# Second chunk of edges in dense tiles: 438 gathers in place of 488, and sums by items of a tile and a block

## The chip, the cores and the metric

One core of a Trainium2 chip runs the whole kernel in one launch. The metric is the device time of that launch in microseconds (us), by the slowest core, and here there is only one.

## What is computed

The reference takes x (6250 nodes of 256 numbers) and 100,000 edges, src and dst. It normalises x, and then adds three things to it: a graph layer, a small attention-like mixer over 8 heads, and at the end a mixture of 8 experts. The graph layer is what this case is about:

```python
def _L0_gnn_ref(x, W1, b1, W2, b2, edge_index):
    dst = edge_index[0]
    nbr = edge_index[1]
    agg = jax.ops.segment_sum(x[nbr], dst, num_segments=n)
    cnt = jax.ops.segment_sum(jnp.ones((nbr.shape[0],), x.dtype), dst, num_segments=n)
    mean = agg / jnp.maximum(cnt, 1.0)[:, None]
    return x @ W1.T + b1 + mean @ W2.T + b2
...
edge_index = jnp.stack([src, dst])
x = x + _L0_gnn_ref(xn, ...) + _L0_mix_ref(xn[None], ...)[0]
x = x + _L0_ffn_ref(_layernorm(x)[None], ...)[0]
```

So row dst[e] of a table is fetched for each edge e and added to the sum of node src[e].

## The kernel before

**Stages.** `edges` normalises x, multiplies it with W2 (by linearity W2 can come before the mean) and stores the products as a table of 6272 rows in HBM, `tab` ("xn_parts", 512 f16 numbers, 1 KB a row). It then sorts the edges on the chip and sums the fetched rows. `nodes` finishes the layer, normalises and routes; `experts` runs the eight experts.

**Sorting.** The 100,000 edges lie as 125 partitions by 800 columns and are handled in two chunks, of 352 and of 448 columns (44,000 and 56,000 edges). A block is 128 nodes, and there are NB = 49 blocks. Each edge of a chunk gets a place: a tile and a lane of 128. A block begins on a new tile, so a chunk has room for 49 partly empty tiles: `chunk_plan` (L46) makes 392 tiles for the first chunk (T0 = 392) and 488 for the second. Places that no edge has hold zeros after the sort, which stands for row 0 of the table; behind the last block's last tile whole tiles are left over. By the numbers, 56,000 edges fill 437.5 tiles, and with half a tile lost in each of 49 blocks some 462 of the 488 hold edges.

The steps of a sort are: count (L638, mask products), `place` (L963, VectorE: running sums, where each block's tiles begin), `rank` (L990), `split`, one column after another (L677 on TensorE, L1101 and L1106 on VectorE, L569 on ScalarE), and `decode` (L1025), which leaves `idx`, the table's row for each place, and `srcl`, the node's lane in the block. `buck` says for each tile which block it is of.

**Summing.** For tile t GpSimd issues one indirect DMA (L471), which fetches 128 rows of 1 KB into one of RING = 32 slots in SBUF; even tiles have their slots in G2 (named w in the profile, since the slots lie in a weight buffer), odd ones in G. It waits for the tile 32 before to be summed. TensorE (`sum_tile`, L684) waits for the slot, and multiplies the tile by a one-hot of `srcl` (S, made by VectorE at L926 for eight tiles at a time) in two matmuls, L697 and L698, into one of four PSUM banks. VectorE (`tile`, L932) adds the bank to the block's sums in XA (L947), at an address from a register; 16 such registers are loaded with one instruction (L936).

```python
    def slot(t):
        return (G, G2)[t % 2], t % RING // 2 * GW
...
        for t in range(TILES):
            if t in (0, T0):
                pool.wait_ge(s_dec, 1 if t == 0 else 2)
            if t >= RING and t % 2 == 0:
                pool.wait_ge(s_tile, t + 2 - RING)
```

**What runs beside the sums.** While the first chunk is summed, its tiles carry the sort of the second: `side_plan` (L107) lists the steps with a cost each and spreads them over the first T0 - RING = 360 tiles. While the second chunk is summed, tiles 16 to 287 of it carry the mixer's head statistics, between tiles 287 and 288 the mixer's matrix is folded into W1 (`key_values`, L1159), and tiles 288 to 483 carry, four tiles to a block, the product of the 49 blocks of x with that W1 ("own": L773, L779, L781 on TensorE, L584 and L587 on ScalarE, L1193 and L1196 on VectorE). For L1196 x is loaded again, by SyncE (L430), up to four blocks ahead.

## Time and profile before

| | |
|---|---|
| median of 3 runs | 2108.47 us (2102.12 to 2109.26) |
| profiled execution, its own time | 2104.35 us |
| its span in the profile | 2102.7 us |
| first gather of the first chunk | 333.4 us into the span |
| gathers of the second chunk | 858.2 to 1492.0 us |
| last add of the second chunk | 1507.1 us |
| busy, of the span | TensorE 75%, VectorE 65%, GpSimd 49%, ScalarE 34% |

Times in the profile count from the span's start. Engines are PE (TensorE), PEld (its weight loads), DVE (VectorE), ACT (ScalarE), POOL (GpSimd), SP (SyncE); a name with q is the engine's instruction queue, where register, semaphore and DMA-issuing instructions show, which are not counted as busy. L471 is line 471 of the kernel before.

### The profile page before, as it was taken

How to read it: one execution, taken by the hardware profiler on the slowest of the kernel's cores; microseconds unless marked ns; L12 is line 12 of the kernel's file. 1: busy time of each engine (PE TensorE's matmuls, PEld its weight loads, DVE VectorE, ACT ScalarE, POOL GpSimd, SP SyncE). 2: the span in 40 equal slices, each digit the busy share in tenths (PEclk: the TensorE clock that was granted, in tenths of full speed). 3: DMA queues.
4: the chain of work that ended last, by engine and by line, in shares of the span. 5: the costliest groups of instructions: out<-in, count | busy, mean ns of one | idle time of the engine just before them, and what ended most of it. 6: DMA issues, size and time to landing. Idle time of an engine off the chain costs nothing. (4 is left out here: it accounts for less than half of the span.)

```text
span 2102.7 us, 24562 instructions
## 1 busy us (share of the span) xinstructions
PE 1578.8 (75%) x6551; PEld 876.4 (42%) x6551; DVE 1362.8 (65%) x3687; ACT 720.3 (34%) x1992; POOL 1023.1 (49%) x1020
## 2 busy tenths in 40 slices
PE   4659896668778875465655667888575799999997
PEld 3434432223333332122222234444374466666665
DVE  6679997789899996466666665555564244444444
ACT  5349992008777873000000001111163122222221
POOL 0000105777777777777777777777336011111111
PEclk9779999679999997555555567766555899999999
DMA  5110162333333335733333344444734422223200
GB/s 150 41 41 21 78 254 63 102 100 96 96 96 101 99 97 103 106 103 102 106 101 103 103 122 124 129 123 114 130 136 159 131 90 89 98 91 101 97 12 5
DMA packets 89244, 210.87 MB, mean 100 GB/s; under 512 B 20674, under 2 KB 49896, under 8 KB 86128
## 3 DMA queue, kind: packets, MB, share of 16 engines
q0 software_dynamic: 51888, 138.08, 25.1%
q1 hardware_dynamic: 35544, 70.56, 10.0%
q8 instruction: 58, 0.95, 0.2%
q10 hardware_dynamic: 1680, 0.67, 0.1%
q14 instruction: 74, 0.61, 0.1%
HBM read 163.98 MB, written 49.89 MB: 102 GB/s over the span
## 5 line engine op out<-in xcount | busy, mean ns | idle before, releaser
L947 DVE TENSOR_TENSOR XA<-XA,bank 128x257 f32 x880 | 368.5, 419 | 341.1 <-PE bank L698 318.8
L471 POOL DMA_INDIRECT G<-xn_parts,idx x440 | 445.3, 1012 | 170.0 <-issue 81.9
L471 POOL DMA_INDIRECT w<-xn_parts,idx x440 | 446.5, 1015 | 134.0 <-issue 134.0
L697 PE MATMUL bank<-G,S 128*128 128x257 f16 x440 | 152.2, 346 | 178.6 <-DMA G<-xn_parts,idx 156.4
L1620 POOL DMA_INDIRECT out<-ob,tok x64 | 66.5, 1039 | 401.3 <-DVE ob L1606 401.3
L697 PE MATMUL bank<-w,S 128*128 128x257 f16 x440 | 151.1, 343 | 138.2 <-DMA w<-xn_parts,idx 120.9
L569 ACT ACTIVATE LV<-LH,v 125x128 f16<-125x128 f16 x600 | 182.6, 388 | 188.0 <-DVE LH L1101 187.7
L1544 PE MATMUL bank<-w,ht 128*117 128x256 f32 (+1 forms) x1024 | 223.7, 379 | 0.0
L1533 PE MATMUL bank<-xt,w 128*128 128x468 f32 (+1 forms) x512 | 215.2, 579 | 0.8 <-ACT xt L1558 0.8
L1544 PEld LDWEIGHTS bank<-w,ht 128*117 128x117 f32 (+1 forms) x1024 | 188.8, 186 | 30.5 <-issue 0.4
L1568 ACT ACTIVATE ht<-bank,b1c 128x468 f32<-128x468 f32 (+1 forms) x128 | 85.6, 669 | 333.8 <-PE bank L1533 333.8
L1597 DVE TENSOR_TENSOR y<-bank,b 128x256 f32<-128x256 f32 (+1 forms) x64 | 27.1, 424 | 235.1 <-PE bank L1544 235.1
L697 PEld LDWEIGHTS bank<-G,S 128*128 128x128 f16 x440 | 46.3, 105 | 311.8 <-DMA G<-xn_parts,idx 277.7
L677 PE MATMUL bank<-HT,LV 125*128 125x488 f16 x600 | 158.6, 372 | 11.3 <-ACT LV L569 9.3
L697 PEld LDWEIGHTS bank<-w,S 128*128 128x128 f16 x440 | 45.8, 104 | 281.1 <-DMA w<-xn_parts,idx 241.1
L698 PE MATMUL bank<-G,S 128*128 128x256 f16 x440 | 155.2, 353 | 0.0
L698 PE MATMUL bank<-w,S 128*128 128x256 f16 x440 | 154.1, 350 | 0.0
L1533 PEld LDWEIGHTS bank<-xt,w 128*128 128x128 f32 x512 | 98.0, 192 | 109.3 <-issue 106.9
L926 DVE TENSOR_TENSOR S<-iota,srcl 128x1024 f16<-128x1024 f16 x110 | 133.8, 1217 | 2.2 <-issue 2.2
L574 ACT ACTIVATE work<-work 128x768 f32<-128x768 f32 (+1 forms) x17 | 13.9, 818 | 351.7 <-DVE work L1139 351.7
L450 POOL DMA_DIRECT2D xn_parts<-G x13 | 10.0, 768 | 237.6 <-DVE G L883 235.7
L563 ACT ACTIVATE LV<-LH,v 125x128 f16<-125x128 f16 x378 | 113.9, 390 | 7.7 <-DVE LH L1070 7.7
(234 smaller groups left out, 2698.1 us busy)
## 6 DMA issues: line engine op xcount, KB each, us to landing
w<-f SPq DMA_DIRECT2D x16, 1024.0 KB, 7.6
expert_rows<-G SPq DMA_DIRECT2D x7, 2048.0 KB, 21.3
xb<-expert_rows SPq DMA_DIRECT2D x8, 1028.0 KB, 11.2
xb<-expert_rows SPq DMA_DIRECT2D x8, 939.7 KB
G<-xn_parts,idx POOLq DMA_INDIRECT x440, 2.8
w<-xn_parts,idx POOLq DMA_INDIRECT x440, 2.8
XA<-x SPq DMA_DIRECT2D x6, 1024.0 KB, 5.7
xn_parts<-G POOLq DMA_DIRECT2D x12, 512.0 KB, 3.6
```

Source lines behind the costliest of these rows:

```text
L471: pool.indirect_dma_start(g[:, o:o + 2 * D], None, tab, bass.IndirectOffsetOnAxis(ap=idx[:, t:t + 1], axis=0)).then_inc(s_g[t % RING], 16)
L563: ins = act.activation(value_slot0(col, n), lane_slots0(col, 1), ACT.Copy, scale=v[0:EP, col:col + 1])
L569: ins = act.activation(value_slot(k, n), lane_slots(k, 1), ACT.Copy, scale=v[0:EP, COLS0 + k:COLS0 + k + 1])
L677: ins = pe.matmul(psV[n][:, 0:CHUNKS[1][3]], value_slot(k, n), tile_slot(k), start=False, stop=False, skip_group_check=True)
L697: pe.matmul(psA[t % AR][:, 0:AGW], lhs, g[:, o + D:o + 2 * D + 1], start=True, stop=True)
L698: pe.matmul(psA[t % AR][:, 0:D], lhs, g[:, o:o + D], start=False, stop=True, skip_group_check=True).then_inc(s_tile, 1)
L926: v.tensor_tensor(S[:, t % SR * P:(t % SR + SB) * P].rearrange("p (j n) -> p j n", n=P), iota_1[:, :].unsqueeze(1).to_broadcast([P, SB, P] ...
L947: v.tensor_tensor(XA[:, ds(o, AGW)], XA[:, ds(o, AGW)], psA[t % AR][:, 0:AGW], ALU.add).then_inc(s_ev, 1)
L1533: ins = pe.matmul(psH[f % 2][:, 0:cols], w1[q][:, k * F + f * P:k * F + (f + 1) * P], xt[n % 2][:, k * TQ * P:k * TQ * P + cols], start=(k ...
L1544: ins = pe.matmul(psY[m % 2][0:rp, 0:D], ht[:, f * TQ * P + m * rp:f * TQ * P + (m + 1) * rp], w2[q][:, f * D:(f + 1) * D], start=(f == 0) ...
L1568: act.activation(ht[:, f * TQ * P:f * TQ * P + cols], psH[f % 2][:, 0:cols], ACT.Relu, bias=b1c[:, e * FT + f:e * FT + f + 1]).then_inc(s_ ...
L1620: pool.indirect_dma_start(out, bass.IndirectOffsetOnAxis(ap=tok[0:rp, s:s + 1], axis=0), ob[0:rp, s * D:(s + 1) * D], None, bounds_check=N ...
```

## The change

The second chunk's edges are placed one behind another, without a new tile for each block: 56,000 edges in DENSE = 438 tiles, all full but the last. A tile can now hold edges of two blocks, so the sum goes by items, one for each pair of a tile and a block in it: ITEMS = 438 + 48 = 486. Both matmuls and the add run once per item, with the one-hot of only that block's lanes. The first chunk stays as it is.

- `place_dense` (VectorE, in place of `place` for this chunk) and `dense_items` (TensorE) work out for each item its tile, its block and its lanes, and for each tile its last item. 12 VectorE instructions become 28. `decode_dense` with `dense_turn` and `dense_pick` brings the sources from the tiles' order into the items' (8 VectorE instructions become 20). The plan's costs for these steps rise, and 2 x GAP = 6 more tiles carry a piece. The one-hots over tiles (L1106 and L677 before) are 440 wide instead of 488.
- In `sum_tile` TensorE takes the slot's address and the number of landed tiles to wait for from registers, which it loads itself, two loads for 16 items.
- The slots are one array in order of tiles.
- SyncE counts: it waits for each tile's landing and adds one to `s_land`, for which TensorE waits; then it waits for the last item of the tile 16 before (a value from a register) and adds one to `s_free`, for which GpSimd waits.
- The loads of x for L1196 move from SyncE to ScalarE, two blocks ahead in place of four.

```diff
-    for cols in (352, 448):
-        tiles = (cols * EP + NB * (P - 1)) // P
+    for cols, padded in ((352, True), (448, False)):
+        tiles = (cols * EP + NB * (P - 1)) // P if padded else -(-cols * EP // P)
...
+T0 = CHUNKS[0][3]
+DENSE = -(-COLS1 * EP // P)
+ITEMS = DENSE + NB - 1
+IW = -(-ITEMS // SB) * SB
+AHEAD = 16
...
-    rank = place + 1
+    rank = place + 3
...
-    costs = [430] * NB + [8000] + [1100] * (NB + RB1) + [700] * 5 + ([1070] + [350] * (LB - 1)) * (COLS1 // LB) + [1300] * REST + [3000]
+    costs = [430] * NB + [3500, 7000, 4000] + [1100] * (NB + RB1) + [700] * 5 + ([1070] + [350] * (LB - 1)) * (COLS1 // LB) + [1300] * REST + [3000]
...
+        if decode < k <= decode + 2 * GAP:
+            k += 1
...
+    ring = kk["w_0"][:, :].bitcast(F16)
+    ring_high = ring[:, D:RING * GW]
+    G2, G = ring[:, 0:GR * GW], ring[:, GR * GW:RING * GW]
...
-        return (G, G2)[t % 2], t % RING // 2 * GW
+        return t % RING * GW
...
-        sp.wait_ge(s_kv, 1)
-        for b in range(NB):
-            if b >= LD:
-                sp.wait_ge(s_x0, b - LD + 1)
-            rows = P if b < NB - 1 else LASTROWS
-            sp.dma_start(xr[b % LD][0:rows, :], x[b * P:b * P + rows, :]).then_inc(s_xr[b % LD], 16)
+        sp.wait_ge(s_rows, 1)
+        last = []
+        for t in range(T0, T0 + DENSE):
+            sp.wait_ge(s_g[t % RING], 16 * (t // RING + 1))
+            sp.sem_inc(s_land, 1)
+            u = t - T0 - AHEAD
+            if 0 <= u < DENSE - RING:
+                if u % GR == 0:
+                    last[:] = nc.values_load_multi_w_load_instructions(
+                        tile_used[:, u:u + GR], engines=[mybir.EngineType.SP], min_val=T0 + 1, max_val=T0 + ITEMS,
+                        skip_runtime_bounds_check_because="a tile is in no more than NB items, the place step counts them")[1]
+                sp.wait_ge(s_tile, last[u % GR] & 1023)
+                sp.sem_inc(s_free, 1)
 
...
-        for t in range(TILES):
+        for t in range(T0 + DENSE):
             if t >= RING and t % 2 == 0:
-                pool.wait_ge(s_tile, t + 2 - RING)
-            g, o = slot(t)
-            pool.indirect_dma_start(g[:, o:o + 2 * D], None, tab,
+                if t < T0 + RING:
+                    pool.wait_ge(s_tile, t + 2 - RING)
+                else:
+                    pool.wait_ge(s_free, t - T0 + 2 - RING)
+            o = slot(t)
+            pool.indirect_dma_start(ring[:, o:o + 2 * D], None, tab,
                                     bass.IndirectOffsetOnAxis(ap=idx[:, t:t + 1], axis=0)).then_inc(s_g[t % RING], 16)
...
+        def again(b):
+            if b >= LD:
+                act.wait_ge(s_x0, b - LD + 1)
+            rows = P if b < NB - 1 else LASTROWS
+            act.dma_start(xr[b % LD][0:rows, :], x[b * P:b * P + rows, :]).then_inc(s_xr[b % LD], 16)
+
+        for b in range(2):
+            again(b)
+
...
+        def dense_items():
+
+            pe.wait_ge(s_ge, 2)
+            pe.matmul(psG[0][:, 0:IW], ones16[0:NB, 0:1].to_broadcast([NB, P]), from_first[0:NB, 0:IW], start=True, stop=True)
+            pe.matmul(psG[1][:, 0:IW], rest16[0:NB, 0:1].to_broadcast([NB, P]), at_first[0:NB, 0:IW], start=True, stop=True)
+            pe.matmul(psV[1][:, 0:IW], rest16[0:NB, 1:2].to_broadcast([NB, P]), at_last[0:NB, 0:IW], start=True, stop=True)
+            pe.matmul(psV[0][0:1, 0:CHUNKS[1][3]], ones16[0:NB, 0:1], from_start[0:NB, 0:CHUNKS[1][3]],
+                      start=True, stop=True).then_inc(s_bk, 1)
+
+        def dense_turn():
+
+            pe.wait_ge(s_ts, 1)
+            for n in range(4):
+                ins = pe.matmul(psG[0][:, n * P:(n + 1) * P], lane_src[:, n * P:(n + 1) * P], ident16, start=True, stop=True)
+            ins.then_inc(s_tr, 1)
+
+        def dense_pick():
+
+            pe.wait_ge(s_trc, 1)
+            for n in range(4):
+                ins = pe.matmul(psG[1][:, 0:IW], src_lane[:, n * P:(n + 1) * P], pick[n], start=(n == 0), stop=(n == 3))
+            ins.then_inc(s_si, 1)
...
         def sum_tile(t):
             if t == 0:
                 pe.wait_ge(s_one, 2)
-            pe.wait_ge(s_g[t % RING], 16 * (t // RING + 1))
+            if t < T0:
+                o = slot(t)
+                pe.wait_ge(s_g[t % RING], 16 * (t // RING + 1))
+            else:
+                i = t - T0
+                if i % GR == 0:
+                    many = min(GR, ITEMS - i)
+                    item[:] = [nc.values_load_multi_w_load_instructions(
+                        row[:, i:i + many], engines=[mybir.EngineType.PE], min_val=low, max_val=high,
+                        skip_runtime_bounds_check_because="an item's tile is one of the DENSE tiles, its slot one of the ring")[1]
+                        for row, low, high in ((item_slot, 0, (RING - 1) * GW), (item_need, 1, DENSE))]
+                o = item[0][i % GR]
+                pe.wait_ge(s_land, item[1][i % GR] & 511)
             if t % SB == 0:
                 pe.wait_ge(s_S, t // SB + 1)
             if t >= AR:
                 pe.wait_ge(s_ev, t - AR + 1)
             lhs = S[:, t % SR * P:(t % SR + 1) * P]
-            g, o = slot(t)
-            pe.matmul(psA[t % AR][:, 0:AGW], lhs, g[:, o + D:o + 2 * D + 1], start=True, stop=True)
-            pe.matmul(psA[t % AR][:, 0:D], lhs, g[:, o:o + D], start=False, stop=True, skip_group_check=True).then_inc(s_tile, 1)
+            pe.matmul(psA[t % AR][:, 0:AGW], lhs, ring_high[:, ds(o, AGW)], start=True, stop=True)
+            pe.matmul(psA[t % AR][:, 0:D], lhs, ring[:, ds(o, D)], start=False, stop=True, skip_group_check=True).then_inc(s_tile, 1)
 
...
+        pe.wait_ge(s_sid, 1)
         for h in range(2):
             pe.matmul(psG[h][:, 0:KW], zero32[:, :], W1[:, 0:KW], start=True, stop=False, skip_group_check=True)
-        for t in range(T0, TILES):
+        pe.wait_ge(s_rows, 1)
+        for t in range(T0, T0 + ITEMS):
...
+            step(v.tensor_tensor(starts[0:NB, 1:2], starts[0:NB, 0:1], lanes[0:NB, 0:1], ALU.add))
+            v.tensor_scalar(from_start[0:NB, 0:tiles], iota_t[0:NB, 0:tiles], starts[0:NB, 0:1], None, ALU.is_ge)
+            wait()
+            step(v.tensor_scalar(starts[0:NB, 2:3], starts[0:NB, 1:2], 1.0, None, ALU.subtract))
+            v.tensor_scalar(from_first[0:NB, 0:IW], iota_t[0:NB, 0:IW], starts[0:NB, 1:2], None, ALU.is_ge)
+            v.tensor_scalar(at_first[0:NB, 0:IW], iota_t[0:NB, 0:IW], starts[0:NB, 1:2], None, ALU.is_equal)
+            wait()
+            v.tensor_scalar(at_last[0:NB, 0:IW], iota_t[0:NB, 0:IW], starts[0:NB, 2:3], None, ALU.is_equal).then_inc(s_ge, 1)
+            yield
...
+            step(v.tensor_scalar(keep, psG[1][:, 0:IW], lanes[:, 0:1], None, ALU.is_le))
+            v.scalar_tensor_tensor(out=item_tile, in0=psG[0][:, 0:IW], scalar=-1.0, in1=iota_t[:, 0:IW],
+                                   op0=ALU.mult, op1=ALU.add)
+            v.tensor_scalar(buck[0:1, T0:T0 + IW], psG[0][0:1, 0:IW], -1.0, float(RW), ALU.add, ALU.mult)
+            wait()
+            v.scalar_tensor_tensor(out=keep, in0=psV[1][:, 0:IW], scalar=lanes[:, 1:2], in1=keep,
+                                   op0=ALU.is_gt, op1=ALU.mult)
+            step(v.scalar_tensor_tensor(out=used16[0:1, :], in0=psV[0][0:1, 0:tiles], scalar=float(T0),
+                                        in1=iota_t[0:1, 0:tiles], op0=ALU.add, op1=ALU.add))
...
+            v.wait_ge(s_ts, 1)
+            for n in range(4):
+                v.tensor_scalar(pick[n], item_tile, lanes[:, 2 + n:3 + n], None, ALU.is_equal)
+            v.wait_ge(s_tr, 1)
+            v.tensor_copy(src_lane, psG[0][:, 0:4 * P]).then_inc(s_trc, 1)
...
+            v.sem_inc(s_rows, 1)
+            v.wait_ge(s_si, 1)
+            v.tensor_tensor(srcl[:, T0:T0 + IW], psG[1][:, 0:IW], keep, ALU.mult).then_inc(s_sid, 1)
```

TensorE at the start of the second chunk's sums, before (L697, L698: the two matmuls of a tile, G and w the slots):

```order
L784 MATMUL bank<-W,zero 128x129 x2
L697 MATMUL bank<-G,S 128x257 [waits tile_added,source_onehot,gathered_8]
L698 MATMUL bank<-G,S 128x256
L697 MATMUL bank<-w,S 128x257 [waits tile_added,gathered_9]
L698 MATMUL bank<-w,S 128x256
```

and now (L777 loads 16 registers, L782 masks one, ISA sets an address):

```order
L882 MATMUL bank<-W,zero 128x129 [waits item_sources]
L882 MATMUL bank<-W,zero 128x129
L777 TENSOR_LOAD v [waits item_rows_ready]
L777 TENSOR_LOAD v
L782 REGISTER_ALU
L788 ISA [waits tile_added,source_onehot,tiles_landed]
L788 MATMUL bank<-w,S 128x257
L789 ISA
L789 MATMUL bank<-w,S 128x256
L782 REGISTER_ALU
L788 ISA [waits tile_added,tiles_landed]
L788 MATMUL bank<-w,S 128x257
```

Three instructions of the queue come to each item, two loads to each 16, and the wait for one slot's own semaphore has become a wait for the count of landed tiles.

SyncE's queue behind its last loads of the sort, before:

```order
L424 DMA cum<-gb 128x256
L430 DMA work<-x 128x256 [waits key_values_in_w1]
L430 DMA work<-x 128x256 x3
L430 DMA work<-x 128x256 [waits x_added_again] x44
L430 DMA work<-x 106x256 [waits x_added_again]
```

and now (a piece from its middle):

```order
L467 REGISTER_ALU [waits tile_summed,gathered_6]
L467 REGISTER_ALU [waits tile_summed,gathered_7]
L464 TENSOR_LOAD pos [waits tile_summed,gathered_8]
L467 REGISTER_ALU
L467 REGISTER_ALU [waits tile_summed,gathered_9]
L467 REGISTER_ALU [waits tile_summed,gathered_10]
```

The 49 loads have left this queue, and for every tile it waits in turn for a landing and for a sum.

## Rows read from the trace of the kernel before

**Rows 1.** The page: the span

```profile
span 2102.7 us, 24562 instructions
```

**Rows 2.** Groups of instructions, POOL, 858.1 to 1493 us

```profile
L471 POOL DMA_INDIRECT G<-xn_parts,idx x244 | 246.5, 1010 | 74.3 <-PE bank L698 40.2 <-issue 34.1
L471 POOL DMA_INDIRECT w<-xn_parts,idx x244 | 239.9, 983 | 74.3 <-issue 74.3
```

**Rows 3.** Timeline of POOL, the second chunk's first and last gather

```profile
858.19 0.95 POOL L471 DMA_INDIRECT G<-xn_parts,idx  x1 [0.30 <-issue]
...
1492.03 0.95 POOL L471 DMA_INDIRECT w<-xn_parts,idx  x1 [0.30 <-issue]
```

**Rows 4.** Stretches: busy us (count) of PE, PEld, DVE, ACT, POOL; clock, DMA share, GB/s

```profile
858.10:1228.70 370.60, 215.20 (x790) 93.48 (x790) 223.16 (x450) 17.67 (x34) 282.79 (x289) 0.52 0.39 105
1228.70:1460.00 231.30, 184.66 (x698) 104.70 (x698) 129.51 (x303) 29.99 (x87) 178.08 (x175) 0.71 0.44 126
1460.00:1508.00 48.00, 35.53 (x107) 17.69 (x106) 20.25 (x46) 3.82 (x11) 25.57 (x25) 0.50 0.81 81
820.00:858.00 38.00, 14.32 (x50) 3.35 (x48) 15.63 (x32) 0.00 (x0) 29.05 (x30) 0.50 0.92 92
500.00:800.00 300.00, 238.52 (x1227) 103.12 (x1226) 277.58 (x739) 236.87 (x782) 232.39 (x223) 1.00 0.35 98
1360.00:1370.00 10.00, 10.00 (x32) 6.00 (x30) 4.59 (x10) 0.89 (x3) 7.56 (x9) 0.50 0.46 132
```

**Rows 5.** Timeline of a gather, its matmuls and its add, mid second chunk

```profile
1003.68 0.94 POOL L471 DMA_INDIRECT G<-xn_parts,idx  x1 [0.30 <-PE bank L698]
...
1006.76 0.40 PE L697 MATMUL bank<-G,S 128*128 128x257 f16 x1 [0.53 <-DMA G<-xn_parts,idx]
...
1007.50 0.42 DVE L947 TENSOR_TENSOR XA<-XA,bank 128x257 f32 x1 [1.15 <-PE bank L698]
```

**Rows 6.** Timeline of the second chunk's last tiles

```profile
1505.72 0.40 PE L697 MATMUL bank<-G,S 128*128 128x257 f16 x1 [1.21 <-DMA G<-xn_parts,idx]
...
1507.09 0.42 DVE L947 TENSOR_TENSOR XA<-XA,bank 128x257 f32 x1 [0.20 <-DVE XA L947]
```

**Rows 7.** The lines of the gather (L471), its time to landing

```profile
  issue: 216.0, 709
...
DMA to landing us min/median/max: 2.6/2.8/15.4
```

**Rows 8.** Queue of DVE: loads of 16 registers (L936)

```profile
L936 DVEq TENSOR_LOAD <-buck x56: 594/1099/1344, 332.6 to 1496.2; - x56
```

**Rows 9.** Queue of DVE: the register instruction before each add (L947)

```profile
L947 DVEq FUSED_REGOPS  x880: 46/46/46, 337.0 to 1507.0; - x176
```

**Rows 10.** Timeline of PE, one "own" block from L779 to L779

```profile
1360.20 1.91 PE L779 MATMUL bank<-W,work 128*128 128x256 f32 x4
...
1365.30 1.91 PE L779 MATMUL bank<-W,work 128*128 128x256 f32 x4
```

**Rows 11.** Timeline of PE, behind key_values, and POOL's gather for the first of them

```profile
1228.68 0.95 POOL L471 DMA_INDIRECT G<-xn_parts,idx  x1 [0.30 <-PE bank L698]
...
1239.03 0.40 PE L697 MATMUL bank<-G,S 128*128 128x257 f16 x1 [5.26 <-DVE mcol L1189]
...
1247.84 1.03 PE L779 MATMUL bank<-W,work 128*128 128x256 f32 x4
...
1250.90 1.03 PE L779 MATMUL bank<-W,work 128*128 128x256 f32 x4
```

**Rows 12.** Issue of L430 by SP

```profile
L430 SPq DMA_DIRECT2D work<-x x49: 258/328/463, 1239.0 to 1477.0; - x49
```

**Rows 13.** Timeline of DVE, `place` of the second chunk

```profile
367.18 1.09 DVE L965 TENSOR_TENSOR_SCAN cum<-onesw,bank 113x448 f32<-113x448 bf16 x1 [0.49 <-PE bank L638]
...
371.48 0.65 DVE L987 TENSOR_SCALAR buck<-bank 1x488 int32<-1x488 f32 x1
```

**Rows 14.** DVE's tile one-hots of the second chunk (L1106)

```profile
L1106 DVE TENSOR_SCALAR HT<-iota_t,tf x300: 327/339/534, 470.5 to 810.9; 125x488 f16<-125x488 f16 x150
```

More of the change, by code:

```diff
@@ L126, with done_at @@
 SIDE, PLACE, RANK, SORT, DECODE = side_plan()
-PLACE_AT = next(t for t in range(T0) if SIDE[t] > PLACE)
-DECODE_AT = next(t for t in range(T0) if SIDE[t] > DECODE)
+def done_at(k):
+    return next(t for t in range(T0) if SIDE[t] > k)
+PLACE_AT, ITEMS_AT, TURN_AT, PICK_AT = (done_at(k) for k in (PLACE, PLACE + 1, DECODE, DECODE + GAP))
 def side_by(t, first, n):
@@ L305, in edges @@
     DI = HT[:, :].bitcast(I32)
-    idx = sb("idx", [P, TILES], I32)
-    srcl = sb("srcl", [P, TILES], F16)
-    buck = sb("buck", [1, TILES], I32)
+    idx = sb("idx", [P, T0 + CHUNKS[1][3]], I32)
+    srcl = sb("srcl", [P, T0 + IW], F16)
+    buck = sb("buck", [1, T0 + IW], I32)
+    lanes = sb("lanes", [P, 6], F32)
+    starts = sb("starts", [P, 4], F32)
+    rest16 = sb("rest16", [P, 2], F16)
+    from_first, at_first, at_last, from_start = (HT[:, n * TMAX:(n + 1) * TMAX] for n in range(4))
+    item_tile = v1[:, 0:IW // 2].bitcast(F16)
+    keep = v2[:, 0:IW // 2].bitcast(F16)
+    used16 = onesw[:, 0:CHUNKS[1][3]].bitcast(F16)
+    item_slot = v1[0:1, EC - IW:EC].bitcast(I32)
+    item_need = v2[0:1, EC - IW:EC].bitcast(I32)
+    tile_used = pos[0:1, 0:CHUNKS[1][3]].bitcast(I32)
+    lane_src, src_lane, ident16 = LV[:, 0:4 * P], LV[:, 4 * P:8 * P], LH[:, 0:P]
+    pick = [HT[:, n * TMAX:n * TMAX + IW] for n in range(4)]
+    assert IW // 2 <= COLS0 and CHUNKS[1][3] <= 4 * P and IW // 2 <= EC - IW
     S = sb("S", [P, SR * P], F16)
@@ L685, in close @@
             ins.then_inc(s_sx, 1)
+        item = []
         def sum_tile(t):
@@ L1091, in second_chunk @@
                 yield
-            place(1, psV[0], psV[1])
+            yield from place_dense()
             yield
```

127 lines of the change are left out of this document (103 added, 24 removed).

## Prediction

> **What bounds the kernel now.** I read the stretches first, then GpSimd's groups, then single tiles in the timeline. The change touches the second chunk's sums, from 858.1 to 1508 us, and the sort steps that ride on the first chunk's. In the second chunk TensorE is busy 215 of 370.6 us, then 185 of 231.3 us, and VectorE less [rows 4]: no compute engine is full. GpSimd issues one indirect DMA after another: 488 of them take 246.5 + 239.9 = 486.4 us, and before each it idles 148.6 / 488 = 0.30 us [rows 2], put down to nothing but its own issue or to a sum long done. It never waits longer. Its pitch is 635.0 / 488 = 1.301 us; an undisturbed gather has 0.95 + 0.30 = 1.25 us [rows 3], and the other 0.05 us is some long ones, met by VectorE's work. TensorE follows: a gather issued at 1003.68 us is multiplied at 1006.76 us behind a wait for the DMA and added at 1007.50 us, 3.8 us after issue [rows 5]. So **the number of gathers times their pitch** bounds this stage, and the tail behind the last one.
>
> That tail is long: the last gather starts at 1492.03 us and the last add at 1507.09 us [rows 3, 6], 15.1 us for what takes 3.8 us elsewhere. From 1460 us the DMA engines are 0.81 busy for 81 GB/s, where before it was 0.39 for 105 GB/s; the same shows at the end of the first chunk, 0.92 for 92 GB/s [rows 4]. These are the stretches in which the left-over empty tiles come, whose 128 lanes all fetch row 0: about 26 of them by the numbers (488 - 462), and the sums then go at the DMA's pace, waiting for it 1.21 us before a tile [rows 6]. I take the empty tiles to be the cause.
>
> **The change, part by part.**
>
> *50 gathers fewer.* If the long ones go in proportion, 50 x 1.301 = 65.1 us; if only undisturbed ones go (VectorE's work per item stays, 486 for 488), 50 x 1.25 = 62.5 us. I take -63.8 us. This counts in full as long as GpSimd sets the pace.
>
> *No empty tiles in the second chunk.* The tail of 15.1 us shrinks. It can't be under 3.8 us; SyncE's hop and the last block's product come on top, and in the stage of the own blocks TensorE runs up to a block late, so I take 7 us: -8 us, with bounds of -11.3 and 0.
>
> *Registers on TensorE.* Two loads for 16 items, and an ALU step and two address steps each. VectorE's load of 16 takes 1.10 us [rows 8], its address step 0.046 us [rows 9]; taken for TensorE, that is 2.2 / 16 + 3 x 0.046 = 0.28 us an item in its queue. Dense, an item comes every 1.301 x 438 / 486 = 1.17 us. In the first 288 items TensorE was busy 0.58 of the time, so 0.65 now, and the queue's part fits even unhidden: 0. In the own stage a block of four items has 4.69 us. Without waits a block takes 5.10 us at the low clock of 1.2 GHz [rows 10] and 3.06 us at 2.4 GHz [rows 11]; the mean granted clock there was 0.71, so 0.42 of the time at the higher level [rows 4]. It ran at 1.2 GHz while it was full from 1360 to 1370 us [rows 4] and got the higher level behind such stretches; a tighter pace leaves fewer waits between them. With everything hidden but half of the loads (0.28 us a block), a block needs 5.38 or 3.34 us, and a third of the time at 2.4 GHz is enough for 4.69 us. I take +2 us for moments when it lags, with bounds 0 and +24 us (first rival). 
>
> *SyncE's counting.* A hop before each sum, some 0.1 to 0.2 us as a wait and a register step cost on VectorE's queue (0.046 us a step [rows 9]), and a load of 1.1 us once in 16 tiles. It delays and doesn't add up, since there are 1.30 us for each tile: 0, and its share of the tail is counted above. Queued behind the wait for a sum is the next landing's count; it would hold TensorE back only with 16 tiles outstanding, and the worst lag was 10.4 us, 8 tiles, behind `key_values` [rows 11]. GpSimd gets a slot back only when the tile 16 later has landed, so it can be 16 ahead: landing takes 2.8 us in the median and 15.4 us at most [rows 7], 12 tiles. No stall of GpSimd from either.
>
> *Loads of x on ScalarE.* 49 issues at 0.33 us by SyncE's row [rows 12]; ScalarE is busy 30 of 231 us there [rows 4], and two blocks ahead are 9 us. 0.
>
> *Sort steps on the first chunk.* 28 more VectorE instructions. `place` took 367.2 to 372.1 us for its 12 [rows 13], 0.4 us each, so some 11 us more, while the tile one-hots get 448 x 0.339 x 48 / 488 = up to 15 us cheaper [rows 14]. VectorE is 0.93 busy there [rows 4], but GpSimd may run 30 tiles ahead, about 40 us, so a lag of 10 to 15 us is covered by the ring. If that cover were gone, the 11 us would be paid. I take +1 us (bounds -3 and +11).
>
> Sum: -63.8 - 8 + 2 + 1 = -68.8 us. The profiled execution had 2104.35 us (span 2102.7 us [rows 1], the rest lies around it), so 2035.6 us. The median of the runs is 4.1 us above that execution: **2040 us**. The later stages are as before.
>
> **Rivals.**
>
> *TensorE bounds the own stage.* Nothing of the register work is hidden and the clock stays where it was: a block takes 5.10 + 1.1 = 6.2 us low and 3.06 + 1.1 = 4.2 us high, together 1 / (0.58 / 6.2 + 0.42 / 4.2) = 5.17 us, against the 4.69 us of the gathers: 49 x 0.48 = 24 us of the gain are given back, 2064 us. For it: the busy share there is already 0.80. Against: the granted clock rose behind full stretches, and at the higher level a block takes 3.06 us [rows 11], so that TensorE soon caught up behind `key_values`.
>
> *Slower than before: loads on TensorE's queue.* TensorE never runs past a register load, and the loads cost it far more than VectorE. The 486 items must then end later than 1507 us. With 288 items at 1.17 us (337 us), the stage breaks even when a block takes (1507 - 858 - 337 - 7) / 49 = 6.2 us all through, so 1.1 us of unhidden register work at the low clock and never the higher one. At three times VectorE's price (6.6 us for two loads, 1.65 us a block, and 0.55 us for the rest) it is 5.10 + 2.2 = 7.3 us: 49 x 1.1 = 54 us over, 2162 us. Against: VectorE loads 16 registers in 1.10 us, and TensorE was at the higher level 0.42 of the time. The Trainium skill (Runtime: NRT & Kernel Launch, "Instruction fetch mechanics") states about 200 ns for each register loaded, so an estimated 3.2 us for 16 and this rival's price; VectorE's row of 1.10 us, 0.07 us a register, speaks against it.
>
> *The gain is lost ahead of it.* VectorE's added steps come on the path of the first chunk (+11 us) and the tail stays (0 for -8): -63.8 + 2 + 11 = -51 us, 2058 us. For it: VectorE is 0.93 busy. Against: GpSimd never waited for a sum there.
>
> *It doesn't do what it says.* If the free counts came so late that GpSimd waits for them, its idle before a gather would exceed 0.30 us; a stall of 0.15 us a gather for 406 gathers would take 61 us back: no change, 2101 us. It needs landings of over 20 us, and the longest is 15.4 us.
>
> **How the numbers follow.** Forecast 0.70, TensorE-bound 0.13, lost ahead 0.08, no change 0.02, slower 0.07. The range takes in the forecast's bounds (-65.1 - 11.3 - 3 gives 2029 us) and the first and third rival, with a little for the unknown size of the register work: 2028 to 2072 us, leaving out some 0.18. A change under 0.5%, 10.5 us, can't be told from none: faster 0.91, same 0.02, slower 0.07.
>
> **What would show it.** Right: 438 gathers from about 858 us to about 1430 us at a pitch near 1.30 us with 0.30 us idle; a last add near 1437 us; DMA share without its rise at the end; a mean clock over 0.71 in the own stage. Wrong: GpSimd idle for longer than 0.30 us, put down to SyncE; TensorE without waits for landings in the own stage and still over 5 us a block; loads on TensorE's queue well over 1.1 us; a first gather of the second chunk later than 862 us.

## The result and the profile after

The changed kernel takes 2046.32 us in the median of 4 runs (2044.0 to 2050.91), beside 2105.3 us (2099.47 to 2109.26, 4 runs) of the kernel before, run beside it: a ratio of 0.9724, with a 95% interval of 0.9699 to 0.975. The forecast was 2040 us, the range 2028 to 2072 us. The profiled execution of the change took 2044.0 us, 60.4 us less than the 2104.35 us of the one before; the terms below are read from these two. The first four experiments ran while tiles landed late on their chip (the kernel before at 2264.15 us, 2258.07 to 2270.76 in 19 runs), so each of them is held against runs of the kernel before made beside it, and not against the numbers here.

The page's span and its row of busy times; then stretches of the second chunk (columns as in [rows 4]): the first two answer to its gathers and the tail behind them, the next two to the heads' and the own blocks' part, the fifth to the end of the first chunk:

```profile
span 2042.3 us, 27345 instructions
PE 1529.3 (75%) x6558; PEld 883.5 (43%) x6558; DVE 1362.1 (67%) x3717; ACT 724.3 (35%) x1992; POOL 985.9 (48%) x970
```

```profile
858.30:1440.00 581.70, 389.82 (x1574) 221.94 (x1574) 365.73 (x787) 56.42 (x131) 448.47 (x438) 0.64 0.40 112
1440.00:1446.00 6.00, 3.79 (x17) 2.34 (x15) 3.87 (x10) 0.38 (x1) 0.01 (x1) 0.78 0.08 25
858.30:1207.00 348.70, 203.33 (x789) 109.38 (x788) 221.08 (x450) 17.67 (x34) 269.67 (x260) 0.54 0.37 101
1207.00:1400.00 193.00, 150.90 (x652) 91.06 (x652) 121.60 (x285) 32.45 (x81) 148.27 (x147) 0.82 0.44 129
820.00:858.00 38.00, 15.72 (x59) 4.96 (x57) 17.85 (x39) 0.00 (x0) 29.15 (x30) 0.54 0.88 93
```

GpSimd's second chunk begins at 858.3 us, as in [rows 3], and has 438 gathers in 448.47 us of busy time: 1.024 us for one, where [rows 2] have 486.4 / 488 = 0.997 us. That is the one number here that went the wrong way. Behind the last gather the DMA engines are 0.08 busy. The first chunk, which still has its empty tiles, ends as before at 0.88 for 93 GB/s. The granted clock in the own blocks' stretch is 0.82, where [rows 4] had 0.71.

The gather's line in the second chunk (first and last start, idle time before it by what ended it, time to landing):

```profile
L512 POOL DMA_INDIRECT w<-xn_parts,idx x438: 942/949/1997, 858.3 to 1439.1; - x146
...
  issue: 126.8, 416
  SPq L468: 4.9, 16
  PE bank L789: 1.8, 6
...
DMA to landing us min/median/max: 2.6/2.8/14.5
```

The idle times add up to 133.5 us over 438 gathers, 0.30 us each; none is longer than 0.32 us, and the 16 put down to SyncE's free count (L468) are 4.9 / 16 = 0.31 us as well. From the first to the last gather the pitch is 580.8 / 437 = 1.33 us, where the prediction asked for one near 1.30 us. The last gathers of either kernel, from 1460 us before (one of the two lines of the tiles' slots) and from 1407 us after, show what became of the empty tiles' landings:

```profile
L471 POOL DMA_INDIRECT G<-xn_parts,idx x12: 942/946/1837, 1461.3 to 1490.8; - x12
...
DMA to landing us min/median/max: 4.4/10.2/14.9
```

```profile
L512 POOL DMA_INDIRECT w<-xn_parts,idx x26: 945/949/1783, 1406.7 to 1439.1; - x26
...
DMA to landing us min/median/max: 2.7/2.9/4.8
```

```profile
1439.06 0.95 POOL L512 DMA_INDIRECT w<-xn_parts,idx  x1 [0.30 <-issue]
...
1445.31 0.42 DVE L1049 TENSOR_TENSOR XA<-XA,bank 128x257 f32 x1
```

The tail is 1445.3 - 1439.1 = 6.2 us. The register work, on TensorE (16 registers in a load, then one address step a line), on SyncE, and the x loads on ScalarE:

```profile
L777 PEldq TENSOR_LOAD <-v x62: 825/1105/1310, 872.3 to 1436.9; - x62
```

```profile
L788 PEldq FUSED_REGOPS  x486: 46/46/51, 875.5 to 1442.2; - x162
```

```profile
L464 SPq TENSOR_LOAD <-pos x26: 967/971/1192, 882.4 to 1414.6; - x26
```

```profile
L627 ACTq DMA_DIRECT2D work<-x x49: 333/334/500, 1217.6 to 1429.8; - x49
```

The difference of the two executions, stage by stage: the second chunk starts at 858.3 for 858.2 us (+0.1); from its first to its last gather 1439.1 - 858.3 = 580.8 us for 633.8 us (-53.0); the tail 6.2 for 15.1 us (-8.9); behind it 597.0 for 595.6 us (+1.4). Together -60.4 us, all of the gain.

### The profile page after: what moved, and what is told of

Read it like the earlier page. It is cut to its first block and busy times, and to the rows that moved or that the text cites. A ratio compares the mean times of both kernels' runs of the same rounds, so it can differ in the third digit from the quotient of the medians.

```text
span 2042.3 us, 27345 instructions
## 1 busy us (share of the span) xinstructions
PE 1529.3 (75%) x6558; PEld 883.5 (43%) x6558; DVE 1362.1 (67%) x3717; ACT 724.3 (35%) x1992; POOL 985.9 (48%) x970
## 3 DMA queue, kind: packets, MB, share of 16 engines
q8 instruction: 64, 1.05, 0.2%
## 5 line engine op out<-in xcount | busy, mean ns | idle before, releaser
L512 POOL DMA_INDIRECT w<-xn_parts,idx x830 | 854.4, 1029 | 289.0 <-issue 236.3
L788 PE MATMUL bank<-w,S 128*128 (+1 forms) x878 | 292.9, 336 | 280.6 <-SPq L460 134.9
L788 PEld LDWEIGHTS bank<-w,S 128*128 128x128 f16 x878 | 92.6, 105 | 488.8 <-issue 312.6
L789 PE MATMUL bank<-w,S 128*128 (+1 forms) x878 | 297.8, 342 | 0.0
L755 PE MATMUL bank<-HT,LV 125*128 125x440 f16 x600 | 151.2, 356 | 16.2 <-ACT LV L610 10.2
L488 POOL DMA_DIRECT2D xn_parts<-w x13 | 10.0, 769 | 237.0 <-DVE w L985 235.1
L789 PEld LDWEIGHTS bank<-w,S 128*128 128x128 f16 x878 | 94.0, 107 | 33.8 <-issue 7.8
L749 PE MATMUL bank<-HT,LV 125*128 125x392 f16 x378 | 92.2, 340 | 14.6 <-ACT LV L604 9.4
L610 ACT ACTIVATE work<-work,v 125x128 f16<-125x128 f16 x296 | 90.3, 387 | 22.0 <-DVE work L1299 21.9
L1304 DVE TENSOR_SCALAR HT<-iota_t,tf 125x440 f16<-125x440 f16 x300 | 94.6, 342 | 0.0
```

Source lines behind the costliest of these rows:

```text
L512: pool.indirect_dma_start(ring[:, o:o + 2 * D], None, tab, bass.IndirectOffsetOnAxis(ap=idx[:, t:t + 1], axis=0)).then_inc(s_g[t % RING], 16)
L610: ins = act.activation(value_slot(k, n), lane_slots(k, 1), ACT.Copy, scale=v[0:EP, COLS0 + k:COLS0 + k + 1])
L749: ins = pe.matmul(psS[0][n][:, 0:CHUNKS[0][3]], lane_slots0(k, 1) if by else value_slot0(k, n), tile_slot0(k, n if by else 0), start=False ...
L755: ins = pe.matmul(psV[n][:, 0:CHUNKS[1][3]], value_slot(k, n), tile_slot(k), start=False, stop=False, skip_group_check=True)
L788: pe.matmul(psA[t % AR][:, 0:AGW], lhs, ring_high[:, ds(o, AGW)], start=True, stop=True)
L789: pe.matmul(psA[t % AR][:, 0:D], lhs, ring[:, ds(o, D)], start=False, stop=True, skip_group_check=True).then_inc(s_tile, 1)
```

## Why a gather became longer

50 gathers fewer took 53.0 us off, not 63.8. The undisturbed gather is as before, 0.946 us and 0.30 us idle. What grew is the time by which gathers exceed 0.946 us: 486.4 - 488 x 0.946 = 24.8 us before, 448.5 - 438 x 0.946 = 34.1 us after. Call it the excess. GpSimd and VectorE in the timeline, first the kernel before, then the changed one:

```profile
1001.18 0.94 POOL L471 DMA_INDIRECT G<-xn_parts,idx  x1 [0.30 <-PE bank L698]
1001.30 1.22 DVE L926 TENSOR_TENSOR S<-iota,srcl 128x1024 f16<-128x1024 f16 x1
1002.43 0.94 POOL L471 DMA_INDIRECT w<-xn_parts,idx  x1 [0.30 <-issue]
```

```profile
990.67 0.94 POOL L512 DMA_INDIRECT w<-xn_parts,idx  x1 [0.30 <-issue]
991.61 1.22 DVE L1028 TENSOR_TENSOR S<-iota,srcl 128x1024 f16<-128x1024 f16 x1
991.92 1.72 POOL L512 DMA_INDIRECT w<-xn_parts,idx  x1 [0.30 <-issue]
```

A build of one-hots for eight sums (1.22 us on VectorE, two operands in SBUF) doesn't touch the gather that runs when it starts. It holds the next one, which ends about 0.8 us behind the build's end: 991.61 + 1.22 + 0.81 = 993.64 us in the second piece. So a build that starts 0.12 us behind a gather's start costs nothing, and one that starts 0.94 us behind costs 0.78 us.

Other VectorE operations with two operands in SBUF do the same. The heads' statistics have two of them for each group of blocks (L1139 and L1154 before, L1337 and L1352 after), 34 in all, most of 0.95 us. A reduction of the same length that reads one operand (L1331) holds nothing, even where it starts 1.18 us behind a gather's start. Both in the changed kernel:

```profile
942.92 0.95 POOL L512 DMA_INDIRECT w<-xn_parts,idx  x1 [0.30 <-issue]
944.01 0.95 DVE L1337 TENSOR_TENSOR work<-XA,hm 128x768 f32<-128x768 f32 x1
944.17 1.61 POOL L512 DMA_INDIRECT w<-xn_parts,idx  x1 [0.30 <-issue]
```

```profile
902.89 0.95 POOL L512 DMA_INDIRECT w<-xn_parts,idx  x1 [0.30 <-issue]
904.07 0.95 DVE L1331 TENSOR_REDUCE hs<-XA 128x24 f32<-128x768 f32 x1
904.15 0.95 POOL L512 DMA_INDIRECT w<-xn_parts,idx  x1 [0.30 <-issue]
```

In the second chunk 45 gathers before and 75 after are 0.05 us or more over 0.946 us, and every one of them ends 0.81 to 0.83 us behind the end of a two-operand operation. By the operation that they follow, the excess is:

| us of excess behind | before | after |
|---|---|---|
| the 61 builds of one-hots | 22.1 | 21.6 |
| the heads' 34 two-operand operations | 2.6 | 10.9 |
| the rest | 0.1 | 1.6 |

So 8.3 of the 9.3 us lie on the heads' operations, and none on the builds. Before, a tile was a gather and a sum, the work that rides on the sums kept its place against the gathers, and 26 of the 34 started within 0.3 us of a gather's start, where they cost nothing. After, 486 sums go with 438 gathers, the two drift, and 11 of 34 start there. The builds drift too: in the heads' part 24 of 37 started within 0.25 us before and 8 of 37 after, and their excess rose there from 7.9 to 12.4 us; but in the own blocks' part, where most had started late already, it fell from 14.2 to 9.2 us.

The Trainium skill (SBUF — State Buffer, "SBUF: two separate sides") states that a VectorE operation with two inputs in SBUF and a GpSimd operation that reads SBUF take a shared port pair as an exclusive lock, and whoever starts second waits. The trace agrees for the gather behind: two operands hold it, one doesn't. It doesn't show a lock for the whole of a gather: the build at 1001.30 us starts while one runs, and neither is longer. The page's "blocked until DVE-end + ~115 ns" would end the gather's wait there, and the rows show its end 0.81 us behind; how much of that is the gather's own work no row here tells.

The experiments were made for the theory of the builds alone; they leave the heads' operations as they are. Its rivals were that the excess is chance or DMA, that SyncE's free count holds gathers, and that register loads do.

## The experiments

In the first four, with tiles landing late, GpSimd waited for landings in both chunks. In the first chunk of the kernel with spread rows a tile was added 47.3 us behind its gather's issue in the median, where the kernel before has 4.7 us.

**The one-hots left out.** The change, without 59 of the second chunk's 61 builds; the sums there use stale one-hots, so this part of the computation is missing.

```diff
             if t % SB == SB // 2 and t + SB // 2 not in (T0, T0 + IW):
-                source_onehots(t + SB // 2)
+                if t < T0 + SB:
+                    source_onehots(t + SB // 2)
+                else:
+                    v.sem_inc(s_S, 1)
```

> The changed kernel, whose sums of the second chunk keep the one-hots of its first 16 items: 59 of the 61 builds of S there are left out, so the sums are made with stale one-hots. Theory A (a gather that starts while VectorE builds one-hots from two operands in SBUF ends only when the build has ended, and 61 builds lengthen the gathers by some 29 us): the second chunk's gathers take 552 us in place of 580.8, and the kernel is about 29 us faster than the changed one, near 2015 us. Theory B (the long gathers come from the DMA engines or the memory, or from the counting on SyncE): the gathers stay at 575 to 585 us and the time near 2044 us.

Measured: 2221.57 us, ratio 0.9811 (0.9782 to 0.9841). The gathers:

```profile
928.50:1592.00 663.50, 421.29 (x438) 0.60 0.34 97
```

```profile
L512 POOL DMA_INDIRECT w<-xn_parts,idx x438: 940/946/1950, 928.5 to 1590.2; - x146
...
  SPq L468: 128.3, 79
```

The excess is 421.3 - 414.3 = 7 us (34.1 with the builds), as the theory has it, and 5 of the 7 us lie behind the heads' operations. But GpSimd spent 128.3 us in 79 idle stretches behind SyncE's free count, since tiles landed late, and the kernel was far from the 2015 us that were expected. Here the time can't show what a shorter gather is worth.

**One-hots in pieces of four.** The same, with builds of four sums (0.69 us) instead of eight in the second chunk.

```diff
...
-        def source_onehots(t):
+        def source_onehots(t, n=SB):
...
+            if t >= T0 and t % PIECE == 0 and t + LOOK < T0 + IW:
+                source_onehots(t + LOOK, PIECE)
...
```

> The changed kernel, with S of the second chunk built for 4 items at a time in place of 8: 122 builds of about 0.66 us in place of 61 of 1.22 us. Theory A: a build costs a gather only what it reaches over the gather's start, which for a random phase goes with the square of its length, so some 0.1 us a build or 12 us in all in place of 29: the gathers take 562 to 568 us in place of 580.8 and the kernel is 13 to 18 us faster than the changed one. If the cost went with the number of builds it would be slower by as much; if with VectorE's work, 6 us more of it and no change.

Measured: 2221.03 us, ratio 0.9803 (0.9772 to 0.9835), 116.5 us idle behind the free count. The excess is 433.66 - 414.35 = 19 us, 15 us less than the 34 of the result's profile, as expected (13 to 18 us less), and the time is that of the version above: on such a chip the excess only takes the place of waiting.

**Later one-hots in the kernel before.** A statistics operation of some 0.4 us ahead of each build of the second chunk.

```diff
             if t % SB == SB // 2 and t + SB // 2 not in (T0, TILES):
+                if t >= T0:
+                    v.bn_stats(lnst[:, 0:6], XA[:, xcols(0)])
                 source_onehots(t + SB // 2)
```

> The kernel before, with one needless statistics instruction of 0.42 us on VectorE ahead of each build of S in the second chunk. VectorE idles a third of that stage, so by its work nothing changes (theory B: 0 us). Theory A (before, one tile took one gather, and most builds began 0.1 to 0.2 us after a gather's start, where they cost nothing; each 0.1 us later costs the next gather 0.1 us): the 24 builds in that phase cost 0.35 us each, others wrap around; the gathers of the second chunk take 640 to 647 us in place of 633.8, the kernel is 6 to 13 us slower than before.

Measured: 2268.81 us, ratio 1.0007 (0.9992 to 1.0022). The excess was 505.7 - 489 x 0.946 = 43 us (the first row, whose stretch takes in one gather of the first chunk), where the next kernel, whose builds are as before, had 488.7 - 461.6 = 27 us (the second row); the time again didn't show it.

```profile
928.40:1645.00 716.60, 505.72 (x489) 0.60 0.38 99
```

```profile
928.60:1639.00 710.40, 488.73 (x488) 0.60 0.35 100
```

**Empty places spread over the table.** The kernel before, where the empty places of the second chunk fetch different rows, not all row 0.

```diff
...
+            if c:
+                wait()
+                step(v.tensor_scalar(d, iota_t[:, 0:tiles], 12.0, mi1[:, 0:1], ALU.mult, ALU.add))
+                step(v.tensor_scalar(e, b, 0.0, None, ALU.is_equal))
+                wait()
+                step(v.tensor_tensor(d, d, e, ALU.mult))
+                wait()
+                step(v.tensor_tensor(idx[:, ch0:ch0 + tiles], idx[:, ch0:ch0 + tiles], d, ALU.add))
```

> The kernel before, where the empty places of the second chunk fetch rows spread over the table in place of row 0 (four more VectorE instructions in decode). Theory of the prediction (empty tiles are slow since all their lanes fetch one row): the last add comes 6 to 8 us after the last gather in place of 15.1, the DMA engines' share over the last 48 us falls from 0.81 to under 0.5, the kernel is 7 to 9 us faster than before. Rival (TensorE's own blocks make the tail): 15 us stay, no change.

Measured: 2263.07 us, ratio 0.9994 (0.9979 to 1.0009). The tail was 27.7 us beside 29.8 us of the kernel with later one-hots: with tiles landing late the tail is long whatever is fetched, and nothing follows for row 0.

The next four ran on another chip, with the kernel before at 2104.32 us (2100.13 to 2110.12, 9 runs).

**The change unedited.**

> The change itself, unedited. Theory (the gathers' issue on GpSimd sets the pace of the second chunk): that holds where landings come 2.8 us after an issue, and then this is 2046 us beside 2105 of the kernel before. Rival for a chip where the first four kernels ran (kernel before 2264 us, GpSimd idle for 60 to 110 us in the second chunk because tiles land late): this comes to about 2221, like the version with one-hots in pieces of four, since what GpSimd saves it spends in waiting.

Measured: 2046.28 us (2042.49 to 2048.06), ratio 0.9728 (0.9708 to 0.9748): the result again. The excess was 444.84 - 414.35 = 30 us, so it differs by some 4 us from one execution to another; 10.0 us of it lie behind the heads' operations and 19.9 us behind the builds. The tail was 4.1 us and what follows it 599.9 us.

**One-hots in pieces of two.** As in pieces of four, with `PIECE, LOOK = 2, 4` (0.42 us a build).

> The change with the one-hots of the second chunk built two items at a time. Theory (a build of 1.22 us on VectorE lengthens the gather that starts in its course, by up to 1 us, a short one hardly): the lengthening of the second chunk's gathers over 0.945 us falls from 34 us to under 10, and where GpSimd's issue is the bound the kernel takes 2046 - 25 = about 2021 us. Rival (more instructions cost VectorE and the gathers more than they give): 2046 or over. Where tiles land late (kernel before near 2264), lengthening falls too but the waits take its place, and the time stays at 2221 within 0.3%.

Measured: 2029.05 us (2021.77 to 2033.88), ratio 0.9648 (0.9629 to 0.9668), 17.2 us under the change unedited. The gathers' line and stretch:

```profile
857.70:1419.00 561.30, 427.67 (x438) 0.67 0.42 116
```

```profile
L514 POOL DMA_INDIRECT w<-xn_parts,idx x438: 942/946/1638, 857.9 to 1417.8; - x146
```

and a build with the gather behind it:

```profile
991.27 0.95 POOL L514 DMA_INDIRECT w<-xn_parts,idx  x1 [0.30 <-issue]
992.19 0.43 DVE L1032 TENSOR_TENSOR S<-iota,srcl 128x256 f16<-128x256 f16 x1 [0.75 <-issue]
992.52 0.95 POOL L514 DMA_INDIRECT w<-xn_parts,idx  x1 [0.30 <-issue]
```

The build starts 0.92 us behind the gather's start, about where the long build above cost 0.78 us, and costs nothing: it ends 0.10 us into the next gather. The excess fell by 444.84 - 427.67 = 17.2 us, and so did the median, though VectorE has four times as many builds. (That the two agree to the tenth is chance: the profiled execution is the fastest of its five, 7.3 us under the median.) This bears the theory of the builds out. The gain was less than expected (-25, from 34 us of excess to under 10; it was from 30 to 13): what lies behind builds went from 19.9 to 4.7 us, and 8.6 of the 13.3 us left lie behind the heads' operations, which this edit doesn't touch.

**The free count later.** `AHEAD = 28` for 16: SyncE counts a tile free only 28 tiles behind the landed one.

> The change with SyncE's count of a free tile 28 tiles behind its count of landed tiles, not 16: four tiles at most are in flight. Theory: where a landing takes 2.8 us (2.2 gathers) little is lost, 0 to +15 us in the second chunk, all of it as idle time of GpSimd released by SyncE. Where tiles land late (kernel before near 2264), the second chunk gets slower by more, +20 to +100 us. Rival (flight depth has no part): no change in either.

Measured: 2052.69 us (2051.9 to 2055.74), ratio 0.9759 (0.9739 to 0.9779), 6.4 us over the change. The idle time before the gathers:

```profile
  issue: 125.2, 411
  SPq L468: 15.9, 23
  PE bank L789: 1.2, 4
```

The 23 idle stretches put down to SyncE sum to 15.9 us, 9 us over 23 x 0.30. This is how a free count that holds gathers looks, and the change's row has none of it.

**The free count earlier.** `AHEAD = 4`.

> The change with SyncE's free count only 4 tiles behind, so that up to 28 tiles are in flight instead of 16. Theory: no change where a landing takes 2.8 us. Where tiles land late (kernel before near 2264) the change's own second chunk had a pitch of 1.514 us for a gather against 1.456 before, because the free count holds it at 16 tiles in flight: the pitch falls to about 1.46, 438 x 0.05 = 22 us less than e5. Rival: the pitch there has another cause, and the time stays within 5 us of e5.

Measured: 2048.85 us (2047.23 to 2051.28), ratio 0.9736 (0.9716 to 0.9757). The second chunk's gathers:

```profile
L512 POOL DMA_INDIRECT w<-xn_parts,idx x438: 942/946/1987, 865.5 to 1445.2; - x146
```

They take 579.7 us from first to last, against 577.0 us in the change unedited on this chip and 580.8 us in the result's profile. The second chunk also began 5.7 us later than in the change unedited, behind a first chunk that the edit leaves as it is. So nothing is to be gained here, and the 2.6 us between the medians are no more than such differences. Whether 16 costs something where tiles land late, which a pitch of 1.51 us in the two packed kernels there against 1.45 and 1.47 us in the two unpacked ones suggests, stays open: this kernel didn't run in that condition.

The last four ran with the kernel before at 2103.11 us (2100.4 to 2108.44, 15 runs).

**Later one-hots in the kernel before, again.**

> The kernel before with one statistics operation (about 0.4 us) ahead of each build of one-hots in the second chunk, as e2, whose chip had late landings. Theory (a build lengthens the next gather by its start's distance behind the running gather's start, less 0.15 us; in the kernel before, 24 of the 37 builds of the first part start 0.05 to 0.22 us behind it and cost nothing): each of them now starts some 0.4 us later and costs 0.3 us or more, those that started late wrap around: lengthening of the second chunk's gathers from 25 us to 33 to 42 us, span of the gathers 634 -> 642 to 651, kernel 2112 to 2121 us, though it does the same work on a VectorE that is half idle. Rival (the lengthening is chance or DMA, not the phase): 25 us as before, 2105 within 3 us.

Measured: 2107.27 us (2104.77 to 2113.03, 11 runs), ratio 1.0016 (1.0006 to 1.0026): 4.2 us slower.

```profile
860.80:1501.50 640.70, 491.68 (x488) 0.60 0.43 110
```

The excess is 491.68 - 461.65 = 30 us for 25 us. In the heads' part 3 of 37 builds now start within 0.25 us of a gather's start (24 before), and the excess behind builds there is 13.3 us for 7.9 us. So a later phase alone costs something in a kernel that has the same gathers and a VectorE half idle: 1.3 to 5.5 us by the interval of the ratio. The 5 us of excess come from one trace each, and the next kernel's trace, with the builds where they were before, has 19.0 us, so their size shows little. I had expected 8 to 17 us: in the own blocks' part, where 22 of 24 builds started late already, nothing was added (13.0 for 14.2 us).

**Empty places spread, again.**

> The kernel before with the empty places of the second chunk fetching different rows of the table, not the one row 0. Theory (the prediction's reason for the tail: the last 27 tiles are empty and their 128 lanes all fetch one row, so landings take up to 15 us): the tail from the last gather to the last add falls from 15.1 us to under 8, the kernel to 2097. Rival (the tail is the other transfers of that stretch, the changed kernel's tail is shorter for another reason): tail 13 to 16 us, 2105.

Measured: 2090.11 us (2088.88 to 2094.85), ratio 0.9929 (0.9914 to 0.9945), 13.0 us faster, more than expected. From 1460 us to the last gather, to be held against the second piece of the landings above:

```profile
L472 POOL DMA_INDIRECT w<-xn_parts,idx x13: 942/946/1793, 1460.7 to 1492.5; - x13
...
DMA to landing us min/median/max: 2.7/2.8/5.1
```

```profile
1460.00:1492.00 32.00, 25.46 (x95) 14.40 (x94) 17.03 (x39) 3.83 (x11) 24.69 (x25) 0.70 0.38 114
```

The empty tiles land in 2.8 us in the median instead of 10.2, the DMA engines are 0.38 busy for 114 GB/s there, and the tail is 3.4 us. The same number of gathers and bytes: that all lanes fetch one row is the cause of the tail. The tail gives 11.6 of the 13.0 us; the excess was 5.8 us lower too in this trace (19.0 us), which is within what executions differ by.

**Register loads doubled.** The change, with TensorE's two loads for each 16 sums written twice in the source.

```diff
-                        for row, low, high in ((item_slot, 0, (RING - 1) * GW), (item_need, 1, DENSE))]
+                        for row, low, high in ((item_slot, 0, (RING - 1) * GW), (item_need, 1, DENSE),
+                                               (item_slot, 0, (RING - 1) * GW), (item_need, 1, DENSE))]
```

> The change with TensorE's two register loads for each 16 items made twice, four loads of about 1.1 us. Theory (the loads' 68 us lie in TensorE's slack, the gathers set the pace; the term was put at +2 with a bound of +24): 0 to +3 us on 2046. Rival (TensorE's queue holds sums back): +20 us or more, GpSimd idle for over 0.30 us.

Measured: 2044.96 us (2043.1 to 2047.96), ratio 0.9718 (0.9703 to 0.9733), the change's own time. But the second pair, whose registers nothing reads, isn't in the program that ran:

```profile
span 2043.5 us, 27345 instructions
```

```profile
L777 PEldq TENSOR_LOAD <-v x62: 823/1105/1297, 873.9 to 1438.3; - x62
```

These are the 62 loads and the 27345 instructions of the unedited change. So this run says nothing on the price of loads. It is the change once more, on the chip of the last four experiments: its excess is 33.1 us, with 8.9 us behind the heads' operations.

**Pieces of two in both chunks.**

```diff
...
             if t in (0, T0):
-                source_onehots(t)
-            if t % SB == SB // 2 and t + SB // 2 not in (T0, T0 + IW):
-                source_onehots(t + SB // 2)
+                for k in range(0, LOOK, PIECE):
+                    source_onehots(t + k, PIECE)
+            if t % PIECE == 0 and (t + LOOK < T0 or T0 <= t < T0 + IW - LOOK):
+                source_onehots(t + LOOK, PIECE)
```

> The change with the one-hots of both chunks built two items at a time (e6 did it in the second alone, and took 2029). Theory: the first chunk's gathers lose 20 of their 35 us of lengthening too, the second chunk starts some 15 to 20 us earlier, and the kernel takes 2009 to 2014 us. Rival (in the first chunk VectorE is at 0.55 to 0.6 busy with sorting steps beside, and the four times as many instructions delay these): the first chunk's gathers keep over 30 us of lengthening, or the sort ends later and the second chunk's start is set by it: 2025 to 2035.

Measured: 2016.66 us (2015.53 to 2017.96), ratio 0.9581 (0.9568 to 0.9594), the fastest version of the study, 28 us under the change on the same chip (the run of the experiment above).

```profile
L514 POOL DMA_INDIRECT w<-xn_parts,idx x438: 942/946/1737, 850.8 to 1412.4; - x146
```

The second chunk starts at 850.8 us, 10.7 us earlier than in that run (861.5 us), not 15 to 20: the first chunk's excess fell from 38 to 25 us only. Of the 25 us 9 lie behind builds (25 of 38 before); 11.7 lie behind a two-operand operation of the sort (L1302, 0.68 us), which the edit leaves as it is.

## Why the prediction was right, and where a term was mis-sized

The direction, the size and the bound were right: the number of gathers times their pitch sets the second chunk.

- **50 gathers fewer: -63.8 forecast, -53.0 measured. The term that failed**, below its own lower end of 62.5 us. The step that failed is "VectorE's work per item stays", from which I had the excess unchanged or shrinking with the gathers. The work stayed and its cost didn't: it grew by 9.3 us, since what a two-operand operation costs hangs on where in a gather it starts, and the change unlocked the two. 8.3 us of it are the heads' operations (2.6 us before, 10.9 after), which in the kernel before mostly started where they cost nothing. 50 x 1.25 = 62.5 less 9.3 is 53.2 us. Two executions of the same program, the change unedited and the one with the loads written twice, have 10.0 and 8.9 us there, so this is no chance of one trace; the total differs by some 4 us between executions of the change, and the unpacked kernel had 24.8 us, with spread rows 19.0 us. Pieces of two show on the builds that a shorter two-operand operation gives the time back. No run changes the heads' operations or restores the old phase in the changed kernel, so that the growth is theirs is the reading of the traces.
- **The empty tiles' tail: -8 forecast, -8.9 measured.** The cause, one row fetched by all lanes, was shown by spreading the rows. That also shows that some 12 of the change's 59 us could be had without packing. How near -8.9 comes to -8 is partly luck: on the other chip the change had a tail of 4.1 us and 599.9 us behind it. The two together are steadier, 603.2 and 604.0 us for 610.7 us before, so 7 us.
- **Registers on TensorE: +2 forecast, 0 measured**, with loads of 1.105 us and steps of 0.046 us, VectorE's durations as taken. In the own blocks' stretch TensorE was busy 150.9 of 193 us at a granted clock of 0.82, and GpSimd never waited for it. How much more register work would have fitted wasn't measured. The rival at 2064 us assumed that the clock stays at 0.71; it rose. Prices three times VectorE's, the slower rival's condition, are refuted by the load's row: 1.105 us for 16 registers. By the 200 ns a register that the Trainium skill states (Runtime: NRT & Kernel Launch, "Instruction fetch mechanics") it would be an estimated 3.2 us; no row here agrees. The page states it of uncached loads; these read SBUF, so it may be another case.
- **SyncE: 0 forecast and measured.** Idle before gathers never exceeded 0.32 us. Only with the count 28 tiles behind did it cost 9 us of waiting, 6.4 us in the time. Where tiles landed late, GpSimd did wait behind SyncE's count, 128.3 us in the kernel without one-hots. My fourth rival asked for just this, landings of over 20 us, and even so the version in pieces of four took 0.9803 of the kernel before's time.
- **Loads of x on ScalarE: 0**, 49 issues of 0.33 us as taken. **Sort steps on the first chunk: +1 forecast, +0.1 measured** (858.3 for 858.2 us); the gain wasn't lost ahead.
- Behind the tail +1.4 us, which I had at 0. The forecast added 4.1 us from the profiled execution to the median; the change's median lies 2.3 us over its own.

The sum by what was measured: 0.1 - 53.0 - 8.9 + 1.4 = -60.4 us for -68.8 us. The 6.3 us by which the median missed the forecast are the gathers' 10.8 us, less what the other terms and the step to the median gave back.

## What to carry to other kernels

When an engine's issue rate is the bound, look at what lengthens its single instructions, and at the phase: here a VectorE operation with two operands in SBUF cost the gathers nothing or most of its length, by where it started, on an engine that is idle a third of the time. Cutting the builds in pieces of 0.42 us took 17.2 us off. Look at every such operation and not only at the most frequent one: the heads' operations made the growth, and no experiment here touched them. Before repacking data to get rid of padding, let the padding fetch different rows: that alone gave 13.0 us. When an edit should add work, count the instructions in its trace before reading its time. And for n units taken off such a chain, count n undisturbed pitches; whether the disturbances go too, or grow, is a term of its own.

## What the runs showed of the hardware

- A VectorE operation with two SBUF operands (1.22 us for a build, 0.95 us for the heads' ones) lets the running indirect gather finish and makes the next one end 0.81 to 0.83 us behind its own end: 0 to 1.05 us each. This covers all 75 gathers of the changed kernel's second chunk that are 0.05 us or more over 0.946 us. A reduction of 0.95 us with one operand costs a gather nothing. With builds of 0.42 us what lies behind builds falls from 19.9 to 4.7 us.
- Gathers whose 128 lanes all fetch one row landed in 10.2 us in the median instead of 2.8, with the DMA engines 0.81 busy for 81 GB/s; with spread rows they were 0.38 busy for 114 GB/s.
- Tiles can land late for a whole set of runs: the kernel before took 2264.15 us beside the first four experiments and 2103.11 us beside the last four, on the same chip. The gathers kept their 0.946 to 0.949 us in the median, and GpSimd's waits took the difference. Why the landings were late was not found.
